# Cross attention with a residual add: values in one go, sums behind them, six right adds ahead of maxima, weights turned ahead of queries, one more bank

## The chip, the cores and the metric

The kernel runs on one core of a Trainium2 chip. The metric is the device time of one execution in microseconds (us), lower is better. TensorE's engine writes results to PSUM, which is used here as eight banks of 128 x 512 float32; VectorE and ScalarE read them from there. GpSimd doesn't read PSUM in this kernel. SyncE issues all transfers between the device memory and the on-chip memory.

## The reference, cut to what matters

```python
# x, ctx: (32, 512, 512) float32; Wq, Wk, Wv: (512, 512); NH = 16 heads of dk = 32
def _L0_xattn_ref(tgt, memory, Wq, Wk, Wv):
    q = (tgt @ Wq.T).reshape(B, N, NH, dk).transpose(0, 2, 1, 3)
    k = (memory @ Wk.T).reshape(B, N, NH, dk).transpose(0, 2, 1, 3)
    v = (memory @ Wv.T).reshape(B, N, NH, dk).transpose(0, 2, 1, 3)
    scores = jnp.einsum('bhqd,bhkd->bhqk', q, k) * scale
    probs = jax.nn.softmax(scores, axis=-1)
    att = jnp.einsum('bhqk,bhkd->bhqd', probs, v)
    att = att.transpose(0, 2, 1, 3).reshape(B, N, D)
    return tgt + att[0]
```

Only `att[0]` is used, the attention of the first of 32 batches. So the attention is computed for one batch (512 queries, 512 keys, 16 heads), and its result of 512 x 512 is added to all 32 batches of x. Nearly all traffic is x in (32 MB) and the sum out (32 MB).

## The kernel before, in words

**Tiles.** The 512 query rows are cut into four tiles j of 128, and each tile into two halves; half H is 0 to 7, with H // 2 the tile. The 32 batches are cut into 8 groups g of 4. A slot holds one tile of one group (128 partitions x 4 rows x 512, 1 MB); there are 20 slots for 32 loads. Loads 0 to 19 need no store; load n from 20 on replaces load n - 20, and waits until both halves of that slot have been stored. Slots 13 to 19 lie over the raw and turned weights and the context, so their loads wait until TensorE has used these; loads 18 and 19 (`CTX_T`, `WV_T`) wait until the last block of `v_right` is filled. SyncE issues everything in one written order: first weights and loads, then for each half and group `store_half`, and behind the store of group g of an odd half the reload for three groups earlier (LAG = 3; it runs on into the next half). SyncE waits in order, so a store that isn't ready holds up all behind it.

**A half.** A unit is two heads, a half has 8 units, a group of heads (HG = 4) has two. For each half TensorE makes scores in four pairs of units (`score_pair`), VectorE takes each unit's maximum (`unit_max`), ScalarE exponentiates (`exponent`), TensorE transposes the result (`turn_probs`) and ScalarE copies it out (`copy_probs`). `invert_sums` (VectorE), `lay_out_sums` (TensorE) and `copy_inverse` (VectorE) spread the inverses of the softmax sums for two head groups at a time. `sum_group` (TensorE, L435) multiplies the turned probabilities with the values, and `normalize` (VectorE, L761) scales the result into `att_t`, which has two buffers. After two groups `turn_left` transposes the left 256 columns, ScalarE copies them to `att_left`, and GpSimd adds them to the eight slots (L289). After the other two `turn_right` leaves the right 256 columns in a PSUM bank, from which VectorE adds them (`add_right`, L769). A store needs both adds.

**Before half 0.** Context and weights are transposed on TensorE (`turn`, L314) and copied out by ScalarE or VectorE as the list `JOBS` says (what, number, bank, by ScalarE or not). Then come keys, queries and values (`v_left`, `v_right`: 4 blocks each of 128 rows x 256 columns, L337). Counters count the jobs in the order of the list, so a wait for one job is a wait for all before it.

**What sets the order.** Each engine's order is written out by hand: for halves 0 and 1 line by line, from half 2 on by `half(H)`. `TURNS` numbers the uses of two banks (4 and 5) that take turns; use n waits until use n - 2 is copied out. Bank 7 (`ATT_T_BANK`) holds the sums of a head group and the laid-out inverses. Bank 6 (`BACK_BANK`) holds the turned right side until its eight adds are done, and before that the sum of group 3 of half 0. In half 0 of the kernel before, blocks of `v_right` stand between the sums and transposes on TensorE. From half 2 on the right adds of a half are spread over the two halves behind it; those of half 1 are: two after the last `normalize` of half 1, then six among the maxima of half 2. In the last halves TensorE's end is followed by three adds of half 6 and eight of half 7.

Of the kernel before, what the change touches and what calls it, by code (L numbers as in the profile page):

```python
# [19 lines left out]
def cross_attention_add(nc, x, ctx, wq, wk, wv, out):  # L20
# [8 lines left out]
    T = N // P  # L29
# [22 lines left out]
    with ExitStack() as stack:  # L52
# [8 lines left out]
        with ExitStack() as early:  # L61
# [49 lines left out]
                ("x0_t", 0, 1, True), ("wq_t", 3, 3, False), ("wv_t", 0, 2, True), ("wv_t", 1, 6, False),  # L111
                ("q_t", 0, 4, True), ("wv_t", 2, 7, False), ("wv_t", 3, 5, True),
                ("v_left", 0, 6, False), ("v_left", 1, 7, False), ("v_left", 2, 6, False), ("v_left", 3, 7, False),
                ("v_right", 0, 6, False), ("v_right", 1, 6, False), ("v_right", 2, 6, False), ("v_right", 3, 6, False)]
        number = {(what, i): n for n, (what, i, *_) in enumerate(JOBS)}

        TURNS = [(0, 0), (0, 1), (0, 2), (0, 3), (0, 4), (0, 5), (0, 6), (0, LEFT_SIDE), (0, 7)]
        TURNS += [(1, 0), (1, 1), (1, 2), (1, 3), ("x0", 1), (1, 4), (1, 5), ("x0_t", 1), (1, 6), (1, 7), (1, LEFT_SIDE)]  # L120
# [60 lines left out]
        def sum_bank(H, g):  # L181

            last = {(0, HG - 1): BACK_BANK, (HALVES - 1, HG - 1): 0}
            return bank[:, last.get((H, g), ATT_T_BANK), 0:QH]
# [25 lines left out]
        def added_through(H, g):  # L210

            return H * GROUPS + g + 1
# [79 lines left out]
        def _(pe):  # L292
# [66 lines left out]
            def score_pair(H, g):  # L359

                if H % 2 == 0 and g == 0:
                    if H == 0:
                        emptied(pe, "wv_t", C - 1)
                    else:
                        out_of_turn_bank(pe, "q_t", H // 2)
# [39 lines left out]
            def lay_out_sums(H, m):  # L405

                pe.wait_ge(recip_ready, inverses_through(H, m))
                if H == 0 and m == 0:
                    emptied(pe, "v_left", T - 1)
                else:  # L410
                    pe.wait_ge(att_t_ready, sums_through(H, 2 * m) - 1)
# [8 lines left out]
            def sum_group(H, g):  # L420
# [3 lines left out]
                if (H, g) == (0, 0):  # L424
                    emptied(pe, "v_left", T - 1)
                elif (H, g) == (0, HG - 1):
                    emptied(pe, "v_right", T - 1)
                elif (H, g) != (HALVES - 1, HG - 1):
                    if (H, g) == (0, 2):
                        emptied(pe, "v_right", T - 1)  # L430
                    pe.wait_ge(att_t_ready, sums_through(H, g) - 1)
# [106 lines left out]
            pe.wait_ge(wv_loaded, 16)  # L538
            turn("wv_t", 0)
            turn("wv_t", 1)  # L540
            bank_free("q_t", 0)
# [3 lines left out]
            last.then_inc(bank_filled, 1)  # L545
            turn("wv_t", 2)
            turn("wv_t", 3)

# [12 lines left out]
            turn_probs(0, 3)  # L561
            score_pair(0, 3)
            lay_out_sums(0, 0)
            value_chunks("v_right", 0, (0, 1))
            sum_group(0, 0)
            value_chunks("v_right", 0, (2, 3))
            turn_probs(0, 4)
            sum_group(0, 1)
            turn_probs(0, 5)
            value_chunks("v_right", 1, range(C))  # L570
            turn_probs(0, 6)
            turn_left(0)
            value_chunks("v_right", 2, range(C))
            turn_probs(0, 7)
            value_chunks("v_right", 3, range(C))
            lay_out_sums(0, 1)
# [19 lines left out]
            turn_probs(1, 6)  # L596
            turn_probs(1, 7)
            lay_out_sums(1, 1)
            turn_left(1)
            sum_group(1, 2)  # L600
# [13 lines left out]
        def _(act):  # L614
# [72 lines left out]

            for what, i, _, by_act in JOBS[:number["wv_t", C - 1] + 1]:
                if by_act:
                    empty(what, i)  # L690
# [12 lines left out]
            copy_probs(0, 5)  # L703
            exponent(0, 7)
            copy_probs(0, 6)
            copy_left(0)
            copy_probs(0, 7)
# [27 lines left out]
        def _(dve):  # L735
# [36 lines left out]
            def half(H):  # L772
# [3 lines left out]
                def add_before(i):  # L776
                    if H == 2:
                        add_right(1, 2 + i)
                    elif H > 3:
                        add_right(H - 2, 5 + i)  # L780

                def add_after(i):
                    if H > 2:
                        add_right(H - 1, i)
                    elif i < 3:
                        add_right(1, 5 + i)

# [29 lines left out]

            for what, i, _, by_act in JOBS[:number["wv_t", C - 1] + 1]:
                if not by_act:
                    empty(what, i)  # L820
# [9 lines left out]
            unit_max(0, 6)  # L830
            unit_max(0, 7)
            copy_inverse(0, 0)
            normalize(0, 0)
            empty("v_right", 0)
            normalize(0, 1)
            empty("v_right", 1)
            invert_sums(0, 1)
            empty("v_right", 2)
            empty("v_right", 3)
            copy_inverse(0, 1)  # L840
# [26 lines left out]
            normalize(1, 3)  # L867
            add_right(1, 0)
            add_right(1, 1)
            unit_max(2, 0)  # L870
            unit_max(2, 1)
            unit_max(2, 2)
            unit_max(2, 3)

# [31 lines left out]
```

## Time and profile before

| what | us |
|---|---|
| median of 3 runs | 200.22 (200.06 to 200.99) |
| the profiled execution | 201.61 |
| its span | 198.8 |
| TensorE busy (matmul) | 164.2 (83%) |
| VectorE busy | 108.5 (55%) |
| ScalarE busy | 96.1 (48%) |
| GpSimd busy | 79.7 (40%) |
| bytes read and written | 37.75 MB and 33.55 MB, 359 GB/s over the span |

The profiled execution is one run of the program with a hardware profiler. Its span is from the first to the last recorded piece of work. Times in the views are from the start of that span. In the rows PE is TensorE's matmuls and PEld its weight loads, DVE is VectorE, ACT ScalarE, POOL GpSimd, SPq SyncE's queue; L435 is line 435 of the kernel before.

### The profile page before, as it was taken

How to read it: one execution, taken by the hardware profiler on the slowest of the kernel's cores; microseconds unless marked ns; L12 is line 12 of the kernel's file. 1: busy time of each engine (PE TensorE's matmuls, PEld its weight loads, DVE VectorE, ACT ScalarE, POOL GpSimd, SP SyncE). 2: the span in 40 equal slices, each digit the busy share in tenths (PEclk: the TensorE clock that was granted, in tenths of full speed). 3: DMA queues.
4: the chain of work that ended last, by engine and by line, in shares of the span. 5: the costliest groups of instructions: out<-in, count | busy, mean ns of one | idle time of the engine just before them, and what ended most of it. 6: DMA issues, size and time to landing. Idle time of an engine off the chain costs nothing.

```text
span 198.8 us, 5532 instructions
## 1 busy us (share of the span) xinstructions
PE 164.2 (83%) x2216; PEld 108.2 (54%) x2216; DVE 108.5 (55%) x211; ACT 96.1 (48%) x222; POOL 79.7 (40%) x70
## 2 busy tenths in 40 slices
PE   6999997999999996888899998989999999932000
PEld 6945377576884465724557763655947565721000
DVE  0213352435216983277746197679369899839400
ACT  2311143165431982168684576588287878810000
POOL 1000000000069304940049519809906939989100
PEclk9999999999999999999999999999999999985555
DMA  6999999999956987507999989999999999998994
GB/s 232 401 432 424 422 417 422 422 419 422 420 219 227 404 343 300 216 23 232 342 423 415 424 303 320 411 415 365 347 419 418 411 412 412 417 415 360 410 409 169
DMA packets 14824, 71.65 MB, mean 360 GB/s; under 512 B 1616, under 2 KB 1616, under 8 KB 10320
## 3 DMA queue, kind: packets, MB, share of 16 engines
q1 hardware_dynamic: 14800, 71.31, 90.1%
q8 instruction: 17, 0.28, 0.5%
q14 instruction: 7, 0.06, 0.1%
HBM read 37.75 MB, written 33.55 MB: 359 GB/s over the span
## 4 chain that ended last, share of the span: by engine, by line
PE 74%; DVE 9%; issue 7%; ACT 2%; DVEq 1%; POOL 0%; ACTq 0%; POOLq 0%
PE bank L337 15%; PE bank L372 14%; PE bank L384 14%; PE bank L435 9%; PE bank L332 7%; DVE slots L769 5%; PE bank L446 5%; PE bank L314 3%; PE bank L415 3%; PE bank L503 3%; PE bank L320 2%; DVE neg_max L743 1%; ACT probs L630 1%; DVE wq_t L739 1%; DVE att_t L761 1%
## 5 line engine op out<-in xcount | busy, mean ns | idle before, releaser
L289 POOL TENSOR_TENSOR slots<-slots,att_left 128x512 f32<-128x512 f32 x64 | 79.0, 1273 | 104.3 <-ACT att_left L645 104.3
L743 DVE TENSOR_REDUCE neg_max<-bank 128x1 f32<-128x512 f32 x64 | 41.9, 683 | 21.4 <-PE bank L372 21.4
L630 ACT ACTIVATE probs<-bank,neg_max 128x512 f32<-128x512 f32 x64 | 44.9, 702 | 11.2 <-DVE neg_max L743 11.2
L638 ACT COPY probs_t<-bank 128x512 f32<-128x512 f32 x64 | 37.7, 589 | 18.6 <-PE bank L384 18.1
L384 PE MATMUL bank<-ident,probs 128*128 128x128 f32 x256 | 39.4, 281 | 4.7 <-ACT probs L630 4.7
L769 DVE TENSOR_TENSOR slots<-slots,bank 128x512 f32<-128x512 f32 x64 | 41.8, 676 | 0.7 <-PE bank L446 0.7
L384 PEld LDWEIGHTS bank<-ident,probs 128*128 128x128 f32 x256 | 28.1, 141 | 14.7 <-ACT probs L630 10.3
L372 PE MATMUL bank<-k_t,q_t 32*64 32x512 f32 x256 | 34.3, 611 | 0.7 <-ACT q_t L657 0.7
L435 PEld LDWEIGHTS bank<-probs_t,v 128*32 128x32 f32 x1024 | 16.3, 111 | 16.5 <-ACT probs_t L638 8.1
L435 PE MATMUL bank<-probs_t,v 128*32 128x64 f32 x1024 | 21.2, 224 | 4.7 <-issue 3.4
L761 DVE TENSOR_TENSOR att_t<-bank,inverse 128x256 f32<-128x256 f32 x32 | 13.4, 420 | 16.2 <-PE bank L435 16.1
L337 PE MATMUL bank<-wv_t,ctx_t 128*128 128x256 f32 x64 | 16.0, 388 | 1.5 <-ACT wv_t L623 1.4
L332 PE MATMUL bank<-x_t,wq_t 128*128 128x128 f32 x128 | 15.0, 276 | 0.5 <-DVE wq_t L739 0.5
L332 PEld LDWEIGHTS bank<-x_t,wq_t 128*128 128x128 f32 x128 | 14.6, 192 | 0.7 <-issue 0.7
L337 PE MATMUL bank<-ctx_t,wk_t 128*128 128x512 f32 x32 | 14.7, 593 | 0.0
L337 PEld LDWEIGHTS bank<-wv_t,ctx_t 128*128 128x128 f32 x64 | 11.4, 190 | 4.9 <-issue 2.0
L630 ACT ACTIVATION_READ_ACCUMULATOR probs<-bank,neg_max 128x1 f32 x64 | 13.6, 212 | 0.0
L446 PE MATMUL bank<-ident,att_t 128*128 128x128 f32 x64 | 11.0, 294 | 1.4 <-DVE att_t L761 1.1
L415 PEld LDWEIGHTS bank<-ident,recip 128*32 128x32 f32 x256 | 4.3, 108 | 13.0 <-DVE recip L749 9.5
L372 PEld LDWEIGHTS bank<-k_t,q_t 32*64 32x64 f32 x256 | 6.8, 130 | 6.9 <-issue 6.0
L739 DVE COPY v<-bank 128x256 f32<-128x256 f32 x8 | 3.4, 425 | 12.5 <-PE bank L337 12.5
L446 PEld LDWEIGHTS bank<-ident,att_t 128*128 128x128 f32 x64 | 7.1, 145 | 3.9 <-DVE att_t L761 2.3
(39 smaller groups left out, 86.3 us busy)
## 6 DMA issues: line engine op xcount, KB each, us to landing
slots<-in_x_dram SPq DMA_DIRECT2D x32, 1024.0 KB, 15.2
out_dram<-slots SPq DMA_DIRECT2D x64, 512.0 KB, 8.6
ctx_raw<-in_ctx_dram SPq DMA_DIRECT2D x1, 1024.0 KB, 4.8
wq_raw<-in_L_xattn_Wq_dram SPq DMA_DIRECT2D x1, 1024.0 KB, 8.7
wv_raw<-in_L_xattn_Wv_dram SPq DMA_DIRECT2D x1, 1024.0 KB, 12.4
wk_raw<-in_L_xattn_Wk_dram SPq DMA_DIRECT2D x1, 768.0 KB, 6.5
wk_raw<-in_L_xattn_Wk_dram SPq DMA_DIRECT2D x1, 256.0 KB, 2.7
```

The source lines that it names most:

```text
L289: nc.gpsimd.tensor_tensor(xs, xs, att_left[:, :, :], ALU.add).then_inc(left_added, 1)
L332: last = mm(ps[:, g * P:(g + 1) * P], wq_t[:, c, g * P:(g + 1) * P], x0_t[:, c, :], start=(c == 0), stop=(c == C - 1))
L337: last = mm(job_bank(what, i), weights, moving, start=(c == 0), stop=(c == C - 1))
L372: last = mm(bank[s * QH:(s + 1) * QH, (u + i // 2) % S_BANKS, :], q_t[rows, g, queries], k_t[rows, g, :], start=True, stop=True, tile_posi ...
L384: last = nc.tensor.transpose(turn_bank(H, u)[:, t * P:(t + 1) * P], probs[:, u % 2, t * P:(t + 1) * P], ident[:, :])
L435: last = mm(sum_bank(H, g)[i * DK:(i + 1) * DK, :], v[:, t, h * DK:(h + 1) * DK], probs_t_of(H, 2 * g + i // 2)[:, t, s * QH:(s + 1) * QH] ...
L446: last = nc.tensor.transpose(ps[:, at:at + P], queries, ident[:, :])
L630: nc.scalar.activation(probs[:, u % 2, :], bank[:, u % S_BANKS, :], ACT.Exp, bias=neg_max[:, H % 2, u:u + 1], scale=1.0, accum_out=row_sum ...
L638: nc.scalar.copy(probs_t_of(H, u), turn_bank(H, u).rearrange("p (t n) -> p t n", t=T)).then_inc(act_turned_out, 1)
L743: nc.vector.tensor_reduce(neg_max[:, H % 2, u:u + 1], bank[:, u % S_BANKS, :], AX_X, ALU.max, negate=True).then_inc(max_ready, 1)
L761: nc.vector.tensor_tensor(att_t[:, g % 2, :, :], sum_bank(H, g).unsqueeze(2).to_broadcast([P, QH, BATCHES]), inverse[:, g, :].unsqueeze(2) ...
L769: nc.vector.tensor_tensor(xs, xs, right_bank(H).rearrange("p (r d) -> p r d", r=HALF), ALU.add).then_inc(right_added, 1)
```

## The change

Three lists and four engines' orders are edited; nothing that is computed changes. `score_pair(0, 0)` waits for the queries' copy in place of the last value weight's. `JOBS` puts the last two value-weight turns ahead of the queries, and `v_right` alternates between banks 6 and 7. In half 0 all four `v_right` blocks stand ahead of `lay_out_sums(0, 0)`, which waits until the last is copied out; `turn_left(0)` moves ahead of the turn of unit 6. Sum (1, 3) goes to bank 6 and waits for the eight right adds of half 0 and no longer for the normalization before it. `turn_left(1)` moves ahead of `lay_out_sums(1, 1)`. VectorE does six right adds of half 1 ahead of the maxima of half 2, and the last two where the first two of the spread adds stood.

```diff
-                ("q_t", 0, 4, True), ("wv_t", 2, 7, False), ("wv_t", 3, 5, True),
+                ("wv_t", 2, 7, False), ("wv_t", 3, 5, True), ("q_t", 0, 4, True),
-                ("v_right", 0, 6, False), ("v_right", 1, 6, False), ("v_right", 2, 6, False), ("v_right", 3, 6, False)]
+                ("v_right", 0, 6, False), ("v_right", 1, 7, False), ("v_right", 2, 6, False), ("v_right", 3, 7, False)]
-        TURNS = [(0, 0), (0, 1), (0, 2), (0, 3), (0, 4), (0, 5), (0, 6), (0, LEFT_SIDE), (0, 7)]
+        TURNS = [(0, 0), (0, 1), (0, 2), (0, 3), (0, 4), (0, 5), (0, LEFT_SIDE), (0, 6), (0, 7)]
...
-            last = {(0, HG - 1): BACK_BANK, (HALVES - 1, HG - 1): 0}
+            last = {(0, HG - 1): BACK_BANK, (1, HG - 1): BACK_BANK, (HALVES - 1, HG - 1): 0}
... (sum_group)
+                elif (H, g) == (1, HG - 1):
+                    pe.wait_ge(right_added, added_through(0, GROUPS - 1))
... (TensorE's order)
-            turn("wv_t", 0)
-            turn("wv_t", 1)
+            for t in range(T):
+                turn("wv_t", t)
             bank_free("q_t", 0)
             emptied(pe, "wq_t", C - 1)
             for g in range(HG):
                 last = make_queries(job_bank("q_t", 0), g)
             last.then_inc(bank_filled, 1)
-            turn("wv_t", 2)
-            turn("wv_t", 3)
...
             score_pair(0, 3)
+            for t in range(T):
+                value_chunks("v_right", t, range(C))
             lay_out_sums(0, 0)
-            value_chunks("v_right", 0, (0, 1))
+            turn_probs(0, 4)
             sum_group(0, 0)
-            value_chunks("v_right", 0, (2, 3))
-            turn_probs(0, 4)
+            turn_probs(0, 5)
             sum_group(0, 1)
-            turn_probs(0, 5)
-            value_chunks("v_right", 1, range(C))
+            turn_left(0)
             turn_probs(0, 6)
-            turn_left(0)
-            value_chunks("v_right", 2, range(C))
             turn_probs(0, 7)
-            value_chunks("v_right", 3, range(C))
             lay_out_sums(0, 1)
...
             turn_probs(1, 7)
+            turn_left(1)
             lay_out_sums(1, 1)
-            turn_left(1)
... (VectorE's order, half(H))
                 def add_before(i):
-                    if H == 2:
-                        add_right(1, 2 + i)
-                    elif H > 3:
+                    if H > 3:
                         add_right(H - 2, 5 + i)
+                    elif H == 2 and i < 2:
+                        add_right(1, GROUPS - 2 + i)
 
                 def add_after(i):
                     if H > 2:
                         add_right(H - 1, i)
-                    elif i < 3:
-                        add_right(1, 5 + i)
...
             normalize(1, 3)
-            add_right(1, 0)
-            add_right(1, 1)
-            unit_max(2, 0)
-            unit_max(2, 1)
-            unit_max(2, 2)
-            unit_max(2, 3)
+            for g in range(GROUPS - 2):
+                add_right(1, g)
+            for u in range(4):
+                unit_max(2, u)
```

ScalarE copies the left side of half 0 ahead of the probabilities of unit 6, and VectorE copies the four `v_right` blocks one after another ahead of `copy_inverse(0, 0)`.

## Rows read from the trace of the kernel before

**Rows 1.** Page, DMA queues: packets, MB, share of 16 engines' span.
```profile
q1 hardware_dynamic: 14800, 71.31, 90.1%
```
**Rows 2.** Stretches: length, busy us (count) of each engine, TensorE's clock, DMA share, GB/s.
```profile
57.00:62.00 5.00, 4.37 (x99) 3.35 (x97) 1.45 (x4) 0.58 (x1) 5.00 (x5) 1.00 0.21 57
84.00:89.00 5.00, 4.22 (x36) 1.57 (x32) 3.26 (x6) 3.19 (x8) 2.90 (x3) 1.00 0.00 1
98.00:115.00 17.00, 16.32 (x267) 11.53 (x268) 8.48 (x20) 11.26 (x29) 9.87 (x8) 1.00 1.02 424
116.00:117.00 1.00, 0.60 (x20) 0.27 (x16) 1.00 (x3) 1.00 (x4) 0.00 (x0) 1.00 0.35 143
122.00:180.00 58.00, 51.44 (x934) 33.48 (x933) 43.38 (x91) 39.15 (x95) 41.10 (x35) 0.98 1.02 404
180.00:182.00 2.00, 0.74 (x4) 0.34 (x2) 2.00 (x5) 0.00 (x0) 2.00 (x2) 0.50 0.70 285
182.00:195.80 13.80, 0.00 (x0) 0.00 (x0) 4.14 (x7) 0.00 (x0) 2.77 (x3) 0.50 1.01 405
```
**Rows 3.** Timeline of SyncE's queue: start, length, line, transfer, count.
```profile
60.15 1.18 SPq L224 DMA_DIRECT2D slots<-in_x_dram  x2
...
115.72 0.54 SPq L230 DMA_DIRECT2D out_dram<-slots  x1
...
118.77 16.63 SPq L230 DMA_DIRECT2D out_dram<-slots  x9
```
**Rows 4.** Timeline ahead of the values; in brackets idle time before, and its releaser.
```profile
27.46 1.04 PE L314 MATMUL bank<-ident,wv_raw 128*128 128x128 f32 x8
28.99 3.81 PE L332 MATMUL bank<-x_t,wq_t 128*128 128x128 f32 x32 [0.49 <-DVE wq_t L739]
...
35.03 1.97 PE L337 MATMUL bank<-wv_t,ctx_t 128*128 128x256 f32 x8 [1.36 <-ACT wv_t L623]
...
33.71 1.07 ACT L623 COPY wv_t<-bank 128x512 f32<-128x512 f32 x1 [0.28 <-PE bank L314]
```
**Rows 5.** Chain of waits in half 0: start, length, what.
```profile
47.22 1.02 PE bank L372 x8
...
53.22 1.73 PE bank L337 x8
...
57.59 0.44 DVE v L739
...
60.94 1.10 PE bank L435 x64
```
**Rows 6.** Timeline of half 0, TensorE and ScalarE.
```profile
60.05 0.43 PE L415 MATMUL bank<-ident,recip 128*32 128x64 f32 x16
...
55.90 0.59 ACT L645 COPY att_left<-bank 128x512 f32<-128x512 f32 x1
```
**Rows 7.** Chain of waits at the end of half 1.
```profile
77.02 0.44 DVE att_t L761
...
77.59 0.69 PE bank L435 x32
...
78.78 0.65 PE bank L446 x4
```
**Rows 8.** Timeline from the end of half 1 to the maxima of half 2.
```profile
74.34 0.66 PE L384 MATMUL bank<-ident,probs 128*128 128x128 f32 x4 [0.24 <-ACT probs L630]
...
79.47 1.29 DVE L769 TENSOR_TENSOR slots<-slots,bank 128x512 f32<-128x512 f32 x2 [0.75 <-PE bank L446]
84.85 2.48 DVE L743 TENSOR_REDUCE neg_max<-bank 128x1 f32<-128x512 f32 x4 [4.09 <-PE bank L372]
...
77.06 9.84 POOL L289 TENSOR_TENSOR slots<-slots,att_left 128x512 f32<-128x512 f32 x8 [10.65 <-ACT att_left L645]
```
**Rows 9.** Chain of waits near TensorE's end.
```profile
174.92 3.12 issue
```
**Rows 10.** DMA queues in 174 to 179 us, columns as in rows 1.
```profile
q8 instruction: 1, 0.02, 1.2%
```

More of the change, by code:

```diff
@@ L362, in score_pair @@
                     if H == 0:
-                        emptied(pe, "wv_t", C - 1)
+                        emptied(pe, "q_t", 0)
                     else:
@@ L408, in lay_out_sums @@
                 if H == 0 and m == 0:
-                    emptied(pe, "v_left", T - 1)
+                    emptied(pe, "v_right", T - 1)
                 else:
@@ L424, in sum_group @@
                 if (H, g) == (0, 0):
-                    emptied(pe, "v_left", T - 1)
-                elif (H, g) == (0, HG - 1):
                     emptied(pe, "v_right", T - 1)
-                elif (H, g) != (HALVES - 1, HG - 1):
-                    if (H, g) == (0, 2):
-                        emptied(pe, "v_right", T - 1)
+                elif (H, g) == (1, HG - 1):
+                    pe.wait_ge(right_added, added_through(0, GROUPS - 1))
+                elif (H, g) not in ((0, HG - 1), (HALVES - 1, HG - 1)):
                     pe.wait_ge(att_t_ready, sums_through(H, g) - 1)
@@ L686, in half @@
                 copy_probs(H, 6)
-            for what, i, _, by_act in JOBS[:number["wv_t", C - 1] + 1]:
+            for what, i, _, by_act in JOBS[:number["q_t", 0] + 1]:
                 if by_act:
@@ L704, in _ @@
             exponent(0, 7)
+            copy_left(0)
             copy_probs(0, 6)
-            copy_left(0)
             copy_probs(0, 7)
@@ L816, in half @@
                 add_after(4)
-            for what, i, _, by_act in JOBS[:number["wv_t", C - 1] + 1]:
+            for what, i, _, by_act in JOBS[:number["q_t", 0] + 1]:
                 if not by_act:
@@ L831, in _ @@
             unit_max(0, 7)
+            for t in range(T):
+                empty("v_right", t)
             copy_inverse(0, 0)
             normalize(0, 0)
-            empty("v_right", 0)
             normalize(0, 1)
-            empty("v_right", 1)
             invert_sums(0, 1)
-            empty("v_right", 2)
-            empty("v_right", 3)
             copy_inverse(0, 1)
```

## The prediction, made before the changed kernel was run

> **What bounds the kernel now.** Three views were read, in this order. First the DMA rows of the page and the stretches [rows 1, 2]: the queue that moves the tensors takes 90.1% of sixteen engines' span, and the stretches say where the missing tenth lies. Loads run without a break to 57 us; then come holes (share 0.21 in 57 to 62, 0.00 in 84 to 89), a full stretch from 98 to 115, a dry point at 116 to 117 (0.35), and from 122 to 195.8 a share of 1.01 to 1.02, broken only at 180 to 182 (0.70). Second, the DMA issues of SyncE [rows 3]: loads of slots 18 and 19 leave at 60.15; the store of group 1 of the third half leaves at 115.72, and behind it the queue is never empty for long. Third, the chain of waits and the timeline of its places [rows 4 to 9]: up to 179 us nearly all of the chain is TensorE, with short hand-overs to VectorE and ScalarE.
>
> So there are two regimes. Up to about 116 us the DMA engines keep finding nothing to do: what they get depends on when right adds are ready, which depends on TensorE. From 116 us on they are the bound: a fixed amount of traffic has to pass. It is started by the stores that TensorE's chain releases at 115.7 us. The end therefore moves by as much as TensorE's chain at 115.7 us moves, provided that the last stores move too. They hang on the same chain: the hole at 180 to 182 is where the last right side becomes ready just after most of the backlog is gone. A hole closed before 98 us is worth nothing by itself, since the queue runs dry at 116 us anyway and waits for the next add.
>
> **The change part by part.** All on TensorE's chain, in the order of the program.
>
> Weights ahead of queries. Before, two value-weight turns start at 27.46, queries start at 28.99 after a wait of 0.49 for VectorE's copy of the query weight and take 3.81 us; the last two turns follow at 32.80 and take until 33.7 (0.44 each); then ScalarE copies for 1.07 us and the values start at 35.03, after 1.36 us of idle TensorE [rows 4]. After: the two turns move up, 0.49 us of them into the wait ahead of the queries. Four turns from 27.46 end at 27.46 + 4 x 0.44 = 29.22; queries take 3.81 us and end at 33.03; ScalarE's wv copy (1.07 us) and VectorE's are done under them. Values start at 33.03 in place of 35.03: 2.00 us gained. The query copy (0.60 us) is hidden under v_left 0, which takes nearly 2 us. Bounds: 1.36 us if only the idle gap before 35.03 goes, 2.2 us if values behind warm queries also run at 1.74 instead of 1.97 us. I take 2.0.
>
> All values in one go, sums behind them. The score pair of units 6 and 7 ends at 47.22 + 1.02 = 48.24, after the change at 46.24. Then four v_right blocks of 1.73 us (the row of 53.22 is one) [rows 5] end at 53.3 (0.1 for starting up). The sums now wait for the last block's copy: 0.02 + 0.44 + 0.14 = 0.60 us, to 53.9. Laying out the sums to the first sum group takes 60.94 - 60.05 = 0.89 [rows 5, 6], with turn_probs 4 in its shade: 54.8. Each normalization between a sum and what needs it costs start to start 78.78 - 77.59 = 1.19 [rows 7], so sum (0,1) starts at 56.0 and turn_left at 57.2 (turn_probs 5 is hidden in the first). turn_left 0.59, the copy of the left side 0.59 on ScalarE, and turn_probs 7 (it needs that bank) starts at 58.4, with turn_probs 6 in the shade; + 0.44, + 0.89 to the last two sum groups at 59.8, + 1.10 = 60.9. The row of before is 60.94 + 1.10 = 62.04. So 13.8 us from that score pair to the end of the half become 14.7: 0.9 of the 2.0 us is given back, because value blocks that filled hand-overs stand ahead of them now. With 0.1 more for hand-overs not seen, 1.0 lost, 1.0 left. Bounds: 0.3 lost (only the wait of 0.60 less the one of the same kind that stands before 58.16 now) and 2.0 (all seven hand-overs of about 0.5, less the 0.93 of idle that was there, plus 0.4). ScalarE's copy of the left side ends near 58.4 instead of 56.49 [rows 6], so GpSimd's left adds start 1.9 us later. That costs nothing while they stay ahead of the right adds (the first of them at 63).
>
> One more bank. Sum (1,3) no longer waits for the normalization of (1,2): 77.02 + 0.44 + 0.14 was the wait [rows 7], so it starts at 76.94 in place of 77.59, and turn_right follows 0.65 to 0.70 sooner. Its new wait, for the eight right adds of half 0, is met (they end at 75.2). Bounds 0 and 0.72; I take 0.7, as the rows on both sides are there. Turning left ahead of laying out: turn_left can start at 75.0, when the turn of unit 7 has issued [rows 8], instead of idling for the reciprocal, and laying out follows 0.4 later than it could; sum (1,2) starts at 76.3 as before. Zero, bounds -0.15 and +0.1. The left side is ready 0.8 us sooner for GpSimd.
>
> Six right adds ahead of the maxima. VectorE did two at 79.47 (1.29 us) and then waited 4.09 us for the scores behind the queries [rows 8]. Four more of 0.60 us are 2.4 us, within 4.09: cost zero; without that cover it would be 2.4. Behind them on VectorE stand the maxima of half 2, for which ScalarE and then TensorE wait; 1.7 us of slack is left. In half 2 VectorE does four adds fewer, but its maxima there wait for TensorE, so I count nothing (bounds 0 and 0.4). What it does for transfers: stores of groups 2 to 5 no longer wait for 88 to 95 us. Their own limit is now the left adds, one per 1.23 us from about 75.3 [rows 8], so the six leave between 78.4 and 82.7. Reloads of slots follow each store by three groups, and they move too. The hole at 84 to 89 closes, and the queue is dry again some 4 us before the next store, whose add keeps its place in half 3. On the end: zero.
>
> Loads of slots 18 and 19 go when v_right 3 is filled: at 53.3 instead of 60.15. That closes 57 to 62 for 5 us of transfer. No compute waits for those slots, and stores then start into an empty queue at 64: zero on the end.
>
> Sum at 115.7 us: 2.0 - 1.0 + 0.7 = 1.7 us earlier. The stores and reloads from there on, and TensorE's end at 179, move by the same 1.7. The profiled execution is 201.61 us, 198.8 of span and 2.8 around it; it becomes 199.9. It lies 1.39 above the median of 200.22, so the forecast is 200.22 - 1.7 = 198.5.
>
> A rule to weigh. The last-but-one stretch of TensorE has a stall of 3.12 us in the middle of 64 equal matmuls, with the clock granted fully until 177.7, and in the same 5 us stands one transfer of 16 KB on the instruction queue [rows 9, 10]. The Trainium skill (Runtime: NRT & Kernel Launch, Instruction fetch mechanics) says that the sequencer fetches 16 KiB blocks ahead and that this is mostly hidden. By the rule the stall is something else and such transfers cost nothing anywhere; by the row one of them can cost 3 us when the queue is full. I side with the row, which makes a rival below.
>
> **The rivals.**
>
> A stall for code, slower. Transfers of the instruction queue stood at 75, 80 and 99 us where the DMA was half empty or near it. The change fills 79 to 102 us, and the loads of slots 18 and 19 fill 57 to 62. If one of these blocks arrives late as at 174.92, the chain loses 3.12 before 116 us: 200.2 - 1.7 + 3.1 = 201.6. It decides from 0.7 us of stall (no change) and from 2.7 (slower). For it: [rows 9, 10]. Against: three blocks passed in 98 to 115 at a share of 1.02 [rows 2] without a stall. With other causes of loss, 0.16.
>
> The gain is eaten. The hand-overs behind the values cost the upper bound of 2.0, or the DMA-bound stretch is disturbed so that its start matters less. Then 0.7 or less is left: 199.5 to 200.4, no change. For it: seven hand-overs in series, where a value block stood in most of them. Against: each has a row. 0.23.
>
> The transfers count in full. The Trainium skill (Perfetto Trace Analysis, Optimization Strategy) says to find the gaps of the most contended engine and make their causes start sooner; here that is the DMA at 90.1%. As a mechanism of this kernel: 5.0 us at share 0.00 and some 4 at 0.21 close, and if the traffic behind could move up, about 5 us of them would reach the end, 195. Against: the dry point at 116 to 117, and order: the next store waits for an add in half 3 wherever the queue stands. 0.08.
>
> **How the numbers follow.** The forecast case, 197.6 to 199.1, has 0.53; the eaten gain 0.23, the slower case 0.16, the large gain 0.08. A measurement of this kernel tells about 0.5% (1.0 us) from no change; so faster 0.61, same 0.23, slower 0.16. The range leaves out most of the large gain and of the stall: 196.6 to 200.9.
>
> **What would show it.** Right: values start at 33.0, the first score pair of half 1 at 61.0, the queries of tile 1 at 77.7, maxima of half 2 at 83.2 with VectorE idle before them; DMA share near 1 from 79 to 102 and low from 103 to 107; the store of group 1 of half 2 at 114.0; TensorE's end at 178, the last transfer at 194. Wrong: a store at 114.0 without the end moving (the stretch behind isn't fixed), a full queue up to 116 (transfers counted all along), an idle gap marked issue before 116 with an instruction transfer in it, or half 1 starting at 62.

## The result, and the profile after

Over 20 runs of each on the same chips the changed kernel took 199.87 us (198.69 to 201.09) and the kernel before 200.71 (199.93 to 202.63). The ratio is 0.9957, 95% interval [0.9936, 0.9978]: 0.43% faster, about half of the 0.85% forecast. The time lies inside the range, and the size was wrong. Some executions fall into a slower state; each ratio in this document is worked out without them and isn't the quotient of the two medians.

The profiled execution of the changed kernel took 198.69 us, span 195.8. That is the fastest of its 20, while the one of before (201.61) was among the slower of its kernel. The two profiles lie 3.0 us of span apart, the medians 0.84. So the first thing to learn from the profile after is where it may not be believed.

The timeline of the changed kernel up to half 1, to be held against [rows 4 to 7]; columns as there.

```profile
1.52 4.48 PE L501 MATMUL bank<-ident 128*128 128x128 f32 x24 [1.52 <-POOL ident L281]
...
28.18 3.74 PE L332 MATMUL bank<-x_t,wq_t 128*128 128x128 f32 x32
31.76 1.89 PE L337 MATMUL bank<-wv_t,ctx_t 128*128 128x256 f32 x8
33.58 1.95 PE L372 MATMUL bank<-k_t,q_t 32*64 32x512 f32 x16
...
44.82 7.17 PE L337 MATMUL bank<-wv_t,ctx_t 128*128 128x256 f32 x32
52.60 0.43 PE L415 MATMUL bank<-ident,recip 128*32 128x64 f32 x16 [0.61 <-DVE v L732]
...
56.03 0.66 PE L444 MATMUL bank<-ident,att_t 128*128 128x128 f32 x4 [0.54 <-DVE att_t L754]
...
57.45 0.63 PE L384 MATMUL bank<-ident,probs 128*128 128x128 f32 x4 [0.33 <-ACT att_left L638]
...
58.90 1.10 PE L433 MATMUL bank<-probs_t,v 128*32 128x64 f32 x64 [0.46 <-ACT probs_t L631]
59.93 1.09 PE L372 MATMUL bank<-k_t,q_t 32*64 32x512 f32 x8
...
74.33 1.10 PE L433 MATMUL bank<-probs_t,v 128*32 128x64 f32 x64 [0.46 <-ACT att_left L638]
75.96 0.66 PE L444 MATMUL bank<-ident,att_t 128*128 128x128 f32 x4 [0.54 <-DVE att_t L754]
```

The first row is the 24 warm-up transposes. Before they took 5.38 us, here 4.48, with the same instructions: the clock was granted in full from 7.0 us on there and from 4.9 here. The turns of the context (7.29 and 6.27) and all that follows stand 1.02 us earlier by this alone. With it taken out, the first scores (36.93 to 33.58) moved 2.33 us, the first scores of half 1 (61.97 to 59.93) 1.02, and `turn_right` of half 1 (78.78 [rows 7] to 75.96) 1.80. From there to the last half all of TensorE keeps that distance.

VectorE behind half 1, to be held against [rows 8]: six adds in one row, and 1.71 us of the 4.09 of idle left.

```profile
76.66 3.67 DVE L762 TENSOR_TENSOR slots<-slots,bank 128x512 f32<-128x512 f32 x6 [0.75 <-PE bank L444]
82.04 2.48 DVE L736 TENSOR_REDUCE neg_max<-bank 128x1 f32<-128x512 f32 x4 [1.71 <-PE bank L372]
```

SyncE's queue [rows 3] and the stretches [rows 2] of the changed kernel:

```profile
52.02 1.18 SPq L224 DMA_DIRECT2D slots<-in_x_dram  x2
...
112.91 0.54 SPq L230 DMA_DIRECT2D out_dram<-slots  x1
```

```profile
57.00:62.00 5.00, 4.21 (x102) 2.48 (x104) 2.05 (x5) 1.57 (x4) 4.61 (x4) 1.00 1.02 421
79.00:102.00 23.00, 19.70 (x286) 10.72 (x285) 12.91 (x26) 15.71 (x38) 7.87 (x8) 1.00 1.00 390
103.00:107.00 4.00, 4.00 (x51) 3.24 (x44) 2.08 (x4) 1.75 (x5) 4.00 (x4) 1.00 0.04 12
113.00:114.00 1.00, 0.61 (x15) 0.10 (x10) 1.00 (x4) 1.00 (x4) 0.00 (x0) 1.00 0.00 0
119.20:177.00 57.80, 51.16 (x936) 33.15 (x934) 45.82 (x96) 39.17 (x95) 41.00 (x35) 0.99 1.02 405
177.00:179.00 2.00, 0.00 (x0) 0.00 (x0) 2.00 (x4) 0.00 (x0) 2.00 (x2) 0.50 1.03 420
```

Both early holes are closed (0.21 to 1.02 in 57 to 62, and 0.00 to 0.95 in 84 to 89, with 1.00 over 79 to 102), and two later ones opened in their place, 0.04 at 103 to 107 and 0.00 at 113 to 114: the queue is ahead and has nothing to do until the add at 112.9. From 119.2 on it is full as before. The hole at 180 to 182 is gone. TensorE stood for 0.92 us in this execution where it stood for 3.12 before [rows 9], and a second profile of the kernel before, with 1.20 us there, has no such hole either (1.04).

### The profile page after: what moved, and what is told of

The parts are those of the page before. It is cut to its first block, busy times and chain, and to the rows that moved or that the text cites. A ratio compares the mean times of both kernels' runs of the same rounds, so it can differ in the third digit from the quotient of the medians.

```text
span 195.8 us, 5530 instructions
## 1 busy us (share of the span) xinstructions
PE 161.7 (83%) x2216; PEld 106.6 (54%) x2216; DVE 108.7 (56%) x211; ACT 96.3 (49%) x222; POOL 79.7 (41%) x70
## 4 chain that ended last, share of the span: by engine, by line
issue 46%; POOL 40%; DMA 5%; SPq 1%; POOLq 1%
POOL slots L289 40%; DMA slots<-in_x_dram 5%; POOLq L52 1%; SPq L244 0%; SPq L243 0%; SPq L242 0%; SPq L241 0%; POOLq L287 0%
## 5 line engine op out<-in xcount | busy, mean ns | idle before, releaser
L433 PE MATMUL bank<-probs_t,v 128*32 128x64 f32 x1024 | 20.6, 222 | 2.1 <-issue 0.9
L337 PE MATMUL bank<-wv_t,ctx_t 128*128 128x256 f32 x64 | 15.1, 384 | 0.0
L444 PE MATMUL bank<-ident,att_t 128*128 128x128 f32 x64 | 10.4, 285 | 1.9 <-DVE att_t L754 1.6
```

What stands on the lines that cost most here:

```text
L337: last = mm(job_bank(what, i), weights, moving, start=(c == 0), stop=(c == C - 1))
L433: last = mm(sum_bank(H, g)[i * DK:(i + 1) * DK, :], v[:, t, h * DK:(h + 1) * DK], probs_t_of(H, 2 * g + i // 2)[:, t, s * QH:(s + 1) * QH] ...
L444: last = nc.tensor.transpose(ps[:, at:at + P], queries, ident[:, :])
```

## The experiments

The first question was where the missing 0.9 us is: in the stretch behind 116 us, which the forecast held to be of fixed length, or ahead of it, where the two profiles had shown all in place. Four kernels ran on one chip, where the kernel before took 200.87 us (23 runs).

**The changed kernel again.** No edit.

> The changed kernel once more, in company with the three others on one chip. In the two profiles at hand the chain moved 2.81 us by the first scores of half 2, of which 1.02 stood ahead of every edit (24 warm-up matmuls took 4.48 us in place of 5.38), so 1.79 by the edits; the end moved 2.9; the medians of 20 runs moved only 0.84. Theory 1 (the DMA-bound stretch starts with the store of group 1 of half 2 and follows the chain one to one; the two profiles differ by luck in the warm-up): this profile has the first scores of half 2 at 80.9 to 81.9 us and the store's landing and the end move with them; the median is 1.5 to 1.9 us under that of the kernel before. Theory 2 (the DMA-bound stretch is of no fixed length and takes back about half): the median is 0.6 to 1.1 us under, and the profile shows the last transfer less early than the chain.

Measured: 199.96 us (12 runs), ratio 0.9973 [0.9944, 1.0002]. Its profile was again a fast one: 198.2, span 195.5, first scores of half 2 at 80.87.

**Right adds spread as before.**

```diff
 # of the changed kernel
-            for g in range(GROUPS - 2):
-                add_right(1, g)
+            add_right(1, 0)
+            add_right(1, 1)
...
+                    if H == 2:
+                        add_right(1, 2 + i)
... (and the three behind them, as before)
```

> The changed kernel with the right adds of half 1 spread among the maxima of half 2 as before (two ahead, six among). Theory 1: the chain at half 2 is as in the changed kernel, the hole in the transfers at 82 to 87 us opens again, and the time is that of the changed kernel within 0.3 us. Theory 2, in the form that the early stores and reloads disturb what is behind them: 0.5 to 1 us faster than the changed kernel. A third possibility, that the closed hole carries part of the gain: 0.5 or more slower than the changed kernel.

Measured: 200.25 us (12 runs), 0.996 [0.9936, 0.9984]. The time is that of the changed kernel. But the profile has the first scores of half 2 at 81.85, 0.98 later than the changed kernel, though nothing ahead of them differs. The loss stands in one place:

```profile
58.81 1.09 PE L433 MATMUL bank<-probs_t,v 128*32 128x64 f32 x63 [0.46 <-ACT probs_t L631]
60.73 0.24 PE L433 MATMUL bank<-probs_t,v 128*32 128x64 f32 x1 [0.82 <-issue]
```

63 of the 64 matmuls of the last two sum groups of half 0 run, then TensorE waits for nothing that the profile shows. (The bracket counts from the modelled end of the matmul before, so it is 0.2 us or so less than what the chain loses.) The one that is late is the 961st instruction on TensorE's list (counted from 0). The stall near the end [rows 9] stands ahead of the 4546th in every profile; between them are 3585 instructions, 14 blocks of 256 within one. One transfer of the instruction queue carries 16 KB [rows 10], which is 256 instructions if each has 64 bytes. The instruction transfer ahead of this gap started at 58.3 us; in the two profiles of the changed kernel it started at 57.1 and 57.2.

**Values between the sums.**

```diff
 # of the changed kernel: v_right in bank 6 alone, TURNS and waits of half 0 as before, and
-            for t in range(T):
-                value_chunks("v_right", t, range(C))
             lay_out_sums(0, 0)
+            value_chunks("v_right", 0, (0, 1))
+            sum_group(0, 0)
+            value_chunks("v_right", 0, (2, 3))
...
```

> The changed kernel with the blocks of v_right back between the sums of half 0 (bank 6 alone, order and waits as before). The chain lost 1.31 us there between the scores of half 0 and of half 1. Theory 1: chain 1.2 to 1.4 us earlier than the changed kernel at half 2, end and median earlier by the same, 2.9 to 3.2 under the kernel before. Theory 2: the median gains half of that, 0.5 to 0.8, over the changed kernel.

Measured: 197.94 us (6 runs), 0.9861 [0.9828, 0.9895]: 2.0 us faster than the changed kernel beside it, and the best of this batch. From the first scores of half 0 to those of half 1 TensorE needs 25.05 us (34.17 to 59.22) against 26.35 in the changed kernel. So 1.30 of the 2.0 is the order, and 0.7 isn't in these two profiles.

**Weights ahead of queries alone.** 
```diff
 # of the kernel before
-                ("q_t", 0, 4, True), ("wv_t", 2, 7, False), ("wv_t", 3, 5, True),
+                ("wv_t", 2, 7, False), ("wv_t", 3, 5, True), ("q_t", 0, 4, True),
...
-            turn("wv_t", 0)
-            turn("wv_t", 1)
+            for t in range(T):
+                turn("wv_t", t)
```

> The kernel before with one edit: the two value-weight turns ahead of the queries. Theory 1: first scores of half 0 2.3 us earlier (less or more by the warm-up), all behind it too, median 2.0 to 2.4 under the kernel before. Theory 2: the same chain, median 1.0 to 1.4 under.

Measured: 198.43 us (6 runs), 0.9896 [0.9871, 0.9922], 2.1 us by the ratio. This one edit alone beats the whole change. Theory 2 of that batch, that the DMA-bound stretch takes half back, falls with it.

The second batch separated the parts, and tried the gap. The kernel before took 200.59 us beside it (25 runs).

**Late loads.**

```diff
 # of the changed kernel
                 if n == CTX_T or n == WV_T:
                     sp.wait_ge(bank_filled, number["v_right", T - 1] + 1)
+                    sp.wait_ge(att_t_summed, sums_through(0, HG - 1))
```

> The changed kernel with one wait more: loads of slots 18 and 19 leave only when the last sum group of half 0 is done, about 60 us in place of 53. In the run with the right adds spread, TensorE stood for 0.82 us (issue) ahead of the last matmul of that sum group, its 961st instruction, exactly 14 x 256 instructions ahead of the stall near the end (the 4546th); the 16 KB instruction transfer before it started 1.1 to 1.2 us later than in the two profiles of the changed kernel, in the middle of the two early loads. Code theory (most runs of the changed kernel stall there, by 0.8 or more, because the early loads fill the DMA engines; the profiles at hand were lucky): the median is 0.6 to 1.2 us under the changed kernel's 199.96, 199.0 or so, and the runs spread less. Rival (the missing 0.9 us is in the DMA-bound stretch): the same as the changed kernel within 0.3, as the chain isn't touched. Second rival (the closed hole at 57 to 62 was worth something): slower than the changed kernel.

Measured: 199.37 us (8 runs), 0.9923 [0.9883, 0.9962], no gap at the 961st instruction. Two transfers of 1 MB leave 9 us later, the DMA share in 57 to 62 falls from 1.02 to 0.10, and the kernel isn't slower for it.

```profile
57.00:62.00 5.00, 4.21 (x103) 2.80 (x102) 1.36 (x4) 1.66 (x3) 3.91 (x4) 1.00 0.10 36
```

The median is 0.6 us under the 199.96 of the changed kernel, at the edge of what was expected, and on another chip. Against the kernel before it is 1.2 us lower, where the changed kernel was 0.9 lower.

**Adds alone.** 
```diff
 # of the kernel before
-            add_right(1, 0)
-            add_right(1, 1)
+            for g in range(GROUPS - 2):
+                add_right(1, g)
...
-                    if H == 2:
-                        add_right(1, 2 + i)
+                    elif H == 2 and i < 2:
+                        add_right(1, GROUPS - 2 + i)
```

> The kernel before with six right adds of half 1 ahead of the maxima of half 2, nothing else. By the prediction: chain unmoved, hole at 84 to 89 closed, queue dry again before the store of group 1 of half 2, time that of the kernel before within 0.4 us. Rival (transfers count in full): 3 us or more faster. The median of the changed kernel against the one with spread adds was -0.3 on the other chip run, which leaves room for a small gain.

Measured: 201.05 us (12 runs), 1.0013 [0.9986, 1.0039]. The DMA share at 84 to 89 goes from 0.00 to 1.04, and the time stays. The store of group 1 of half 2 leaves at 115.62 (before 115.72).

**Bank alone.** 
```diff
 # of the kernel before
-            last = {(0, HG - 1): BACK_BANK, (HALVES - 1, HG - 1): 0}
+            last = {(0, HG - 1): BACK_BANK, (1, HG - 1): BACK_BANK, (HALVES - 1, HG - 1): 0}
...
+                elif (H, g) == (1, HG - 1):
+                    pe.wait_ge(right_added, added_through(0, GROUPS - 1))
...
+            turn_left(1)
             lay_out_sums(1, 1)
-            turn_left(1)
```

> The kernel before with sum (1, 3) in bank 6 and the left turn of half 1 ahead of laying out, nothing else. Chain 0.7 to 0.8 us earlier from the queries of tile 1 on. If the end follows the chain one to one: 0.7 to 0.8 us under the kernel before. If the DMA-bound stretch takes half back: 0.3 to 0.4.

Measured: 200.45 us (12 runs), 0.9975 [0.9947, 1.0004]. The chain moved 0.72 in its profile (`turn_right` of half 1 at 78.06 in place of 78.78; the warm-up took the same time as before). The interval holds 0.7 us and 0.3 alike, so the time doesn't tell here.

**Sixteen warm-ups.**

```diff
 # of the version with values between the sums
-    WARM_UP = 24
+    WARM_UP = 16
```

> The version with weights ahead of queries, the bank, the adds, and v_right blocks left between the sums (197.94), with 16 warm-up transposes in place of 24. In the profiles the clock was granted in full from 4.3 to 7.0 us on, differently in each run, and TensorE's first real work started at 5.8 to 6.7 us behind the warm-up; the first weight had landed by 3.5. If the warm-up is what stands in the way: start of the context turns at 6.1 us in every run, 0.3 to 1.2 us faster than with 24 and less spread. If the full clock comes later with fewer warm-ups: real work at 1.2 GHz at first and no gain or a loss of up to 1 us.

Measured: 197.20 us (6 runs), 0.9815 [0.9777, 0.9852], the fastest of all. But the spans of its six runs are 195.0 on average, those of the version with 24 warm-ups 195.1: inside the program the shorter warm-up gained nothing that shows. The 0.7 us between the medians lie behind the span (see "What lies behind the span" below).

The list is 16 instructions shorter ahead of the sums, so the 961st is now a weight load in the scores behind them. There the gap stands, 1.02 us, inside a group that takes 1.09 in other profiles (the middle row):

```profile
57.54 1.10 PE L437 MATMUL bank<-probs_t,v 128*32 128x64 f32 x64 [0.46 <-DVE inverse L753]
58.57 2.16 PE L372 MATMUL bank<-k_t,q_t 32*64 32x512 f32 x8
60.66 0.66 PE L448 MATMUL bank<-ident,att_t 128*128 128x128 f32 x4
```

The program moved under it and the gap kept its number in the list. That is what a block of instructions does, and no wait of the program. The loads of slots 18 and 19 are hardly to blame here: they left at 56.76 and the instruction transfer started at 57.25, when the loads before them had filled the DMA engines without a break (share 1.01 from 51 to 56.5). So the first loads can fill the engines enough for a stall, without these two.

Four kernels were then run for their profiles alone, without an edit: the changed kernel twice, the version with values between the sums, and the kernel before.

> The changed kernel, for its profile alone. Code theory: a gap marked issue of 0.6 to 1.5 us near its 961st TensorE instruction, in or just behind the last two sum groups of half 0 (58 to 61 us), with the instruction transfer before it starting at 58 or later; once it is counted out, and the time at which the clock rises is allowed for (half a microsecond for each at which it comes later), the chain at the scores of half 2 is that of the other profiles within 0.1. Rival: no gap, the chain in place, and the missing 0.9 us behind 116 us, between the store of group 1 of half 2 and the last transfer.

> The changed kernel once more, for its profile alone: the same two possibilities. The gap is taken to be a matter of chance; with most runs of the changed kernel 0.7 to 0.9 us slower than its two first profiles say, it should stand in at least one of these two looks.

> The version with v_right blocks between the sums, for its profile alone. It reaches the same place of the program at 59 us, 0.7 us sooner, and the version with 16 warm-ups stood for 1.0 us at its 961st instruction. Code theory: a gap of about 1 us here too, which is why its median (197.94) lies 1.3 over its first profile. Rival: no gap.

> The kernel before, for its profile alone. It comes to the same place at 62 us, when its early loads have long been through. Code theory: no gap at the 961st instruction. Rival: gaps there at random in every kernel, so that they cancel in the comparison.

Measured: the gap stood in both profiles of the changed kernel (its third and fourth), and neither in the version with values between nor in the kernel before. The third, then the fourth:

```profile
59.89 1.09 PE L433 MATMUL bank<-probs_t,v 128*32 128x64 f32 x63 [0.46 <-ACT probs_t L631]
61.54 0.24 PE L433 MATMUL bank<-probs_t,v 128*32 128x64 f32 x1 [0.56 <-issue]
```

```profile
58.92 1.09 PE L433 MATMUL bank<-probs_t,v 128*32 128x64 f32 x63 [0.46 <-ACT probs_t L631]
60.87 0.24 PE L433 MATMUL bank<-probs_t,v 128*32 128x64 f32 x1 [0.86 <-issue]
```

The kernel before runs all 64 through at the same place:

```profile
59.84 1.10 PE L435 MATMUL bank<-probs_t,v 128*32 128x64 f32 x64 [0.46 <-DVE inverse L753]
```

So the code theory missed for the version with values between: its median isn't explained by a gap that was seen. (TensorE stood for 0.1 us at that place there.)

Last, the changed kernel and the one with late loads beside each other, as they were, and a further step down with warm-ups (`WARM_UP = 12` in the version with values between).

> The changed kernel beside its version with late loads of slots 18 and 19 on one chip. Code theory: three of five profiles of this half 0 with early loads had the gap at the 961st instruction, each time 0.8 to 1.1 us; median 199.9, 0.8 to 1.0 under the kernel before.

> The changed kernel with loads of slots 18 and 19 held until the last sum of half 0. Code theory: the transfer of the instructions before the 961st no longer stands among those loads, the gap goes away or gets rare; median 0.4 to 1.0 us under the changed kernel on this chip. Rival (the gap comes from the loads before, which the slowest DMA engine finishes at 59.4 us in either version): no difference, and the profile shows the gap.

> The version with v_right blocks between the sums, with 12 warm-up transposes (16 gave 197.20, 24 gave 197.94). If the chain still gains by a sooner start: context turns at 6.1 as with 16, so nothing more to gain at the start, and the place of the block end moves by another 8 instructions past the scores: 0 to 0.8 us under 197.2. If the clock comes later because TensorE has less to do at first: 0.3 to 1 us over 197.2.

Measured: changed kernel 199.86 us (11 runs), 0.9948 [0.9919, 0.9976], with the gap at its largest (row below). Late loads 199.70 (9 runs), 0.9924 [0.9893, 0.9956], no gap. On this chip, side by side, the medians differ by 0.16 us and the ratios by 0.5, with intervals that overlap. The profile came out as expected and the time didn't: 0.4 to 1.0 was expected of the median. Twelve warm-ups 198.18 (6 runs), 0.9826 [0.9783, 0.987]: no gain over sixteen. The clock rose at 10.6 us there, and the first real transposes of the context waited 1.19 us for their data.

```profile
60.19 1.09 PE L433 MATMUL bank<-probs_t,v 128*32 128x64 f32 x63 [0.46 <-ACT probs_t L631]
62.41 0.24 PE L433 MATMUL bank<-probs_t,v 128*32 128x64 f32 x1 [1.13 <-issue]
```

All profiles with the changed half 0 in one table (us; the second column is from the first scores of half 0 to those of half 1, which takes the warm-up out):

| kernel | instruction transfer starts | scores 0 to scores 1 | gap |
|---|---|---|---|
| changed, profile after | 57.1 | 26.35 | none |
| changed, again | 57.2 | 26.45 | none |
| changed, third | 59.1 | 27.15 | yes |
| changed, fourth | 58.5 | 27.45 | yes |
| changed, beside late loads | 59.9 | 27.72 | yes |
| adds spread (early loads too) | 58.3 | 27.41 | yes |
| late loads | 57.1 | 26.36 | none |
| late loads, beside | 57.3 | 26.35 | none |

Two things can be read from these traces beside the table. First, the gap ends 2.4 to 2.5 us after the start of the transfer in all four profiles that have it, and 2.4 after it in the one with sixteen warm-ups. In the two profiles of the changed kernel without a gap TensorE came to the place at 59.7, only 0.2 us or less after that point.

Second, the change also packs the instructions ahead of that place. In TensorE's compiled list the 256 up to that place take 5.3 us in the changed kernel and 9.4 in the kernel before, where long value matmuls stand among them. The stretch of these 256, changed kernel, then the kernel before:

```profile
54.41:59.73 5.32, 3.94 (x124) 3.06 (x126) 1.29 (x5) 3.34 (x8) 2.34 (x2) 1.00 1.02 420
```

```profile
52.34:61.76 9.42, 8.79 (x137) 7.36 (x129) 2.15 (x7) 3.84 (x9) 5.18 (x5) 1.00 0.60 236
```

Counted from the start of each profile's own such stretch, the transfer began 2.7 and 2.9 us later in the two profiles without a gap, 3.7 to 4.2 in the four with one, and 2.0 and 2.1 with late loads, where the DMA engines ran empty at 57.0 to 57.5 us (share 0.53, then 0.1).

And the end against its trigger, in all 17 profiles of this case: the span less the time at which the store of group 1 of half 2 is issued.

| kernel | store issued | span | difference |
|---|---|---|---|
| before | 115.72 | 198.8 | 83.1 |
| before, second | 114.64 | 197.8 | 83.2 |
| changed, profile after | 112.91 | 195.8 | 82.9 |
| changed, fourth | 114.02 | 196.4 | 82.4 |
| changed, beside late loads | 115.56 | 198.1 | 82.5 |
| weights only | 113.24 | 196.1 | 82.9 |
| adds only | 115.62 | 198.4 | 82.8 |
| values between | 112.21 | 194.7 | 82.5 |
| sixteen warm-ups | 112.59 | 195.5 | 82.9 |
| the other eight | 112.9 to 115.0 | 195.5 to 197.8 | 82.6 to 83.2 |

## Why the prediction was wrong in size

**What bounds the kernel: right, and shown.** The last column of the table above is 82.4 to 83.2 us, whatever was changed ahead of it and however full the queue was earlier. The trigger moved by 3.5 us and the end followed it within 0.8. Nor does the end follow TensorE's own stall near 175 us: with 3.12 us of it the difference is 83.1 in the first profile of the kernel before, with 1.20 it is 83.2 in the second.

The signs that the prediction named came too. With the 1.02 us of the warm-up put back, values start at 32.78 (33.0 was forecast), half 1 at 60.95 (61.0), and the store leaves at 113.93 (114.0).

**Weights ahead of queries: right, a little more.** 2.33 us in place of 2.0. Queries to values took 31.76 - 28.18 = 3.58 in place of 3.81, and values to scores 1.82 in place of 1.90, as TensorE doesn't run dry between them: the upper bound of 2.2 had named it.

**Values in one go: right in kind, a little more.** The forecast took 1.0 back, the profiles 1.31. The wait for the last copy is there (0.61), and the row of hand-overs too; the turn of unit 7 came 1.42 behind `turn_left` instead of 1.2. The upper bound of 2.0 for this loss doesn't come out of its terms: seven times 0.5, less 0.93, plus 0.4 is 3.0. The measured loss lies inside either.

**One more bank, left turned first: right.** 0.78 against 0.7 (alone 0.72, or 0.77 with a start that came 0.05 later taken out). All 64 matmuls of the two sum groups run as one row.

**Six adds ahead, holes closed: right.** Nothing on the chain, the holes closed, and the time unmoved within the interval, 1.0013 for the adds alone.

The sum was 2.0 - 1.0 + 0.7 = 1.7; measured on the chain 2.33 - 1.31 + 0.78 = 1.80. The step that failed is this one, as it was put: "No compute waits for those slots, and stores then start into an empty queue at 64: zero on the end." The loads of slots 18 and 19 leave 8 us earlier and keep the DMA engines full until 62 us. No tensor is waited for there, but TensorE's next block of instructions comes through the same engines. At the same time "All values in one go" brings TensorE to the end of its block in 5.3 us in place of 9.4, which the prediction didn't look at. In four of six profiles with early loads the block came late, and the chain lost 0.80, 1.10, 1.06 and 1.37 us, 0.72 on average over the six. With late loads it was in time in two of two, and it was never late at that place in the kernel before.

The trace showed such a stall for one place ahead of the change [rows 9, 10], and the prediction named it as a rival with 0.16 and a price of 3.1 us, the one row it had; "an idle gap marked issue before 116 with an instruction transfer in it" stood among its signs of being wrong. It was rather a cost of about 1 us that many runs pay. A bound on the loads' step, "up to one such stall", would have made the sum 0.7 lower: 199.2. The rest up to 199.87 is mostly the reference: the forecast started from a median of three runs, 200.22, and twenty runs gave 200.71. The time lies in the band of the rival "the gain is eaten" (199.5 to 200.4), though neither of the two causes that this rival gave was at work; that, and the place inside the range, is luck.

**How much of the missing gain that is.** The chain gained 1.80 us by the edits and lost 0.72 on average to the gap: 1.1 left. The measured gain is 0.8 to 1.1 by the medians of three batches (0.84, 0.91, 1.14) and 0.5 to 1.0 by their ratios (0.86, 0.54, 1.04). So the sum closes. The direct test, late loads, is weaker: 1.2 and 1.3 by the medians and 1.55 and 1.53 by the ratios, which is 0.3 or 0.7 us more than the changed kernel, and on the one chip where both ran 0.16 or 0.5. The intervals are about 0.4 to 0.8 us wide to either side. The timed runs agree with the share and don't show it.

What is shown is the mechanism: the place at a block's end in instruction count, which stayed when the program was shifted by 16 instructions, and the gap that ends 2.4 us after a delayed transfer. That the early loads, and not chance, delayed it rests on eight profiles: the transfer began 2.7 us or more behind the start of its stretch in all six with early loads, and 2.0 and 2.1 behind it in the two with late ones. Those two also came to the place 0.7 us later than the two profiles without a gap, as their full clock came later (6.4 and 6.5 us against 4.9 and 4.4), so part of their margin is that.

**What lies behind the span.** A time is longer than its span by 2.6 to 3.1 us in 13 of the 17 profiles and by 1.8 to 2.0 in the other four: the version with values between (both profiles), the one with sixteen warm-ups and the one with twelve. In each of the 13, and in none of the four, one more transfer of the instruction queue starts 1.9 us behind the end of the span. This is the row of the changed kernel in 195 to 210 us:

```profile
q8 instruction: 1, 0.02, 0.5%
```

With 24 warm-ups an execution falls on the short side now and then, in most kernels here; all twelve runs with sixteen or twelve warm-ups do. Whether the extra transfer is the cause isn't shown. The short end explains two things. The version with values between has a median 1.3 us above its first profile because that execution was one with the short end; its span, 194.7, is only 0.4 under the middle of its six. And sixteen warm-ups beat 24 by 0.7 us although the spans are the same.

**The rule that was weighed.** The Trainium skill (Runtime: NRT & Kernel Launch, Instruction fetch mechanics) calls the fetch mostly hidden. It gives 16 KiB blocks of 256 instructions, and the count of 14 x 256 agrees. "Hidden" holds for most of the 17 transfers inside a span. It doesn't for the one ahead of the 4546th instruction (0.92 to 3.12 us of idle in all 17 profiles), nor in five profiles for the one ahead of the 961st (0.8 to 1.4 us). Both places lie in or just behind a dense row of small matmuls, with the DMA engines full. The other rule of the Trainium skill, to close the gaps of the most contended engine (Perfetto Trace Analysis, Optimization Strategy), speaks of gaps within the regime of interest, and the adds alone show why that matters: 5 us of idle DMA closed ahead of the last dry point, nothing gained that shows, since the queue then waits for a later add.

The best version is weights ahead of queries, the bank, the adds, values left between the sums, and sixteen warm-ups: 197.20 us, 0.9815 [0.9777, 0.9852]. About 0.7 us of that is the shorter end behind the span.

## What to carry to other kernels

Find the last moment at which the bound resource ran dry: here the time from there to the end was the same within 0.8 us in 17 profiles, only what moved that moment counted, and a hole closed earlier was worth nothing. Price each edit alone: here one of four parts was worth more than the whole. Hold the span of each run against its time, since some of a difference can lie outside the program. When transfers are moved earlier, ask whose transfers they now stand beside, instruction blocks too, and look in several profiles at the densest rows of small instructions, since a stall of this kind comes in some executions and not in others.

## What the runs showed of the hardware that was not expected

The clock: the same 24 warm-up transposes took 4.20 to 5.38 us, as the full clock (2.4 GHz) was granted from 4.4 to 7.6 us on, differently from run to run of the same kernel. The first scores moved with it by up to 1.4 us, which a comparison of two profiles must take out first.

The instruction queue: a transfer that started at 57.1 to 57.3 us was in time for a block needed at 60 us; those that started at 58.3 to 59.9 cost the chain 0.8 to 1.4 us. TensorE went on 2.4 to 2.5 us after the transfer's start each time.

The end: one more instruction transfer, 1.9 us behind the span, goes with a time that is 0.6 to 1.3 us longer against the same span.
